# A gated attention kernel: the sums of the softmax inverted in another layout, a sixth subtraction on VectorE, and another order of the prologue

## The reference

```python
xn = (x - mean(x)) / sqrt(var(x) + 1e-5)              # over the 128 columns
Q, K, V = xn @ Wq, xn @ Wk, xn @ Wv                   # 16 heads of 64
A = softmax(Q K^T / 8) V                              # per batch and head
P = gelu(A) @ Wpost
s = xn + P
g = silu(quantised(xn) @ quantised(ffn_w).T + bias)   # blocks of 32, FP6 grid
out = x + s * g
```

## Time and profile before

| What | Value |
|---|---|
| median of 3 runs | 1389.54 us (1388.74 to 1390.49) |
| the profiled execution | 1389.97 us, span of its instructions 1388.2 us |
| TensorE busy | 1351.9 us, 97% |
| VectorE busy | 1129.9 us, 81% |
| GpSimd busy | 1152.7 us, 83% |
| ScalarE busy | 766.7 us, 55% |
| mean granted TensorE clock | 0.994 |

### The profile page before, as it was taken

The page is one execution under the profiler, slowest core; times in us unless marked ns, Lnnn a source line. Parts: engine busy times, 40 slices in busy tenths (PEclk is TensorE's granted clock), DMA queues, the critical chain, the costliest instruction groups (busy, mean ns, idle before and its releaser), DMA issues.

```text
span 1388.2 us, 25953 instructions
## 1 busy us (share of the span) xinstructions
PE 1351.9 (97%) x9810; PEld 736.2 (53%) x9810; DVE 1129.9 (81%) x1563; ACT 766.7 (55%) x1059; POOL 1152.7 (83%) x548
## 2 busy tenths in 40 slices
PE   5899999999999999999999999999999999999998
PEld 2455555555455555555555454555555455555588
DVE  6688888888888888888888898888888888888633
ACT  2355556555556665555556556555555555555583
POOL 1488899889889889888988899898889889988850
PEclk9999999999999999999999999999999999999999
DMA  2011112111111112211111111121111101122284
GB/s 81 17 41 53 52 58 77 42 61 58 58 48 65 55 42 66 69 51 54 64 56 42 64 56 57 48 64 56 42 64 56 47 28 49 63 66 70 84 272 130
DMA packets 70551, 87.60 MB, mean 63 GB/s; under 512 B 30494, under 2 KB 44574, under 8 KB 70428
## 3 DMA queue, kind: packets, MB, share of 16 engines
q1 hardware_dynamic: 70428, 85.95, 19.3%
HBM read 69.66 MB, written 16.25 MB: 62 GB/s over the span
## 4 chain that ended last, share of the span: by engine, by line
PE 88%; DVE 9%; issue 1%; ACT 1%; DMA 0%; POOL 0%; SPq 0%
PE acc L523 29%; PE scores L504 23%; PE peaks L483 12%; PE extra L406 9%; PE scores L513 5%; DVE half_maxes L942 5%; PE extra L419 4%; PE scores L587 4%; PE extra L447 1%; PE extra L454 1%; DVE extra L909 1%; DVE quant_tmp L908 1%; DVE turned_sums L985 0%; ACT x_in L618 0%; PE extra L429 0%
## 5 line engine op out<-in xcount | busy, mean ns | idle before, releaser
L825 POOL TENSOR_TENSOR prob_sum<-prob_sum,probs 128x1024 f32<-128x1024 f32 x384 | 914.7, 2382 | 89.0 <-ACT probs L702 48.0
L942 DVE TENSOR_REDUCE half_maxes<-peaks 128x2 f32<-128x1024 f32 x504 | 616.4, 1223 | 170.1 <-PE peaks L483 164.6
L702 ACT ACTIVATE probs<-scores 128x1024 f32<-128x1024 f32 x357 | 355.2, 1024 | 489.2 <-PE scores L513 485.9
L523 PE MATMUL acc<-probs,vals 128*64 128x512 f32 x2048 | 486.1, 595 | 0.0
L523 PEld LDWEIGHTS acc<-probs,vals 128*64 128x64 f32 x2048 | 139.0, 137 | 234.7 <-issue 225.2
L483 PE MATMUL peaks<-k_hi,q_hi 64*128 64x512 f32 x1008 | 231.9, 455 | 8.9 <-DVE half_maxes L942 8.8
L825 POOL TENSOR_TENSOR prob_sum<-probs 128x1024 f32<-128x1024 f32 x64 | 153.4, 2397 | 87.1 <-ACT probs L702 87.1
L483 PEld LDWEIGHTS peaks<-k_hi,q_hi 64*128 64x128 f32 x1008 | 95.2, 184 | 213.4 <-issue 142.4
L504 PE MATMUL scores<-q_hi,k_hi 64*128 64x512 f32 x1024 | 203.1, 393 | 0.0
L504 PE MATMUL scores<-q_hi,k_lo 64*128 64x512 f32 x1024 | 202.5, 392 | 0.0
L504 PE MATMUL scores<-q_lo,k_hi 64*128 64x512 f32 x1024 | 202.1, 391 | 0.0
(11 more groups left out here) (155 smaller groups left out, 947.1 us busy)
## 6 DMA issues: line engine op xcount, KB each, us to landing
max_rep<-max_scratch SPq DMA_DIRECT2D x62, 512.0 KB, 4.0
inv_sum<-inv_scratch SPq DMA_DIRECT2D x128, 128.0 KB, 2.8
att_scratch<-att SPq DMA_DIRECT2D x48, 256.0 KB, 2.1
probs<-att_scratch SPq DMA_DIRECT2D x8, 512.0 KB, 5.9
max_scratch<-turned SPq DMA_DIRECT2D x252, 1.0 KB
xTs<-att_scratch SPq DMA_DIRECT2D x4, 512.0 KB, 3.5
out_dram<-xn SPq DMA_DIRECT2D x8, 256.0 KB, 3.2
max_rows<-max_scratch SPq DMA_DIRECT2D x126, 2.0 KB
```

The lines of the kernel that those rows point to most:

```text
L523: last = mm(acc[own[h], :], vals[(s // 2) % 2][:, j, own[h]], probs[j][:, h, :], start=(k == 0), stop=(k == KT - 1), tile_position=col[h])
L702: sa.activation(probs[j][:, :, :], src[:, :, :], ACT.Exp, scale=DH ** -0.5).then_inc(probs_ready, 1)
L825: gp.tensor_tensor(prob_sum[s % 2][:, :, :], before[:, :, :], probs[order(s)[j]][:, :, :], ALU.add).then_inc(probs_summed, 1)
L942: v.tensor_reduce(half_maxes[:, :, f // 2, f % 2], peaks[:, :, :], AX.X, ALU.max).then_inc(peaks_read, 1)
```

## The change: what it does

- `BY_VECTOR` gets (0, 4) for odd steps: VectorE also subtracts the maxima of tile 4, in round 2, so six tiles a pair are its own. TensorE leaves out the L513 pair of that tile, and ScalarE takes tile 5 before tile 4.
- The sums lie in SBUF eight to a partition over 128 partitions, not 32 to a partition over 32: the transpose (L981) and its semaphore are gone, the load is two transfers of 64 partitions, each in pieces of 8 values, the addition runs over 128x32 to 128x8 and the inversion over 128x8. The inverses come back in another order, and GpSimd reads them 16 values apart in `normalise`.
- `centre` and `gates` move to the odd step: `centre` in two parts of four tiles, at the end of rounds 2 and 3, and `gates` at the end of round 2, with the following `high` of q put ahead of the second exponential of round 3. `square` moves to round 0 of the next pair's even step.
- The prologue: TensorE runs 18 matmuls on constants into `peaks` before its first transpose; its first peaks and the projections of v are interleaved; VectorE normalises the first half of rows as early as it can, with the weight's blocks and quantisation in the gaps, and reduces four peaks before it makes the lower parts of the second half.

```diff
...
-    sum_d = nc.dram_tensor("sum_scratch", (P // SQ, 2 * HALF // SQ, SQ), F32, kind="Internal").ap()
+    sum_d = nc.dram_tensor("sum_scratch", (2, P // SQ, SQ, HALF // SQ), F32, kind="Internal").ap()
...
-    BY_VECTOR = ((0, 2, 4, 6), (0,))
+    BY_VECTOR = ((0, 2, 4, 6), (0, 4))
...
-        sums, turned_sums = sb("sums", [P, P]), sb("turned_sums", [P, SQ])
-        group_sums, sums_turned, sums_flat = sums[:, 0:SQ], turned_sums[:, :], turned_sums[0:SQ, :]
+        group_sums, sums = sb("group_sums", [P, 2 * HALF // SQ]), sb("sums", [P, P // SQ, 2 * HALF // P])
+        sums_flat = sb("sums_flat", [P, 2 * HALF // P])
...
-        group_summed, folded = sem("group_summed"), sem("folded")
+        group_summed = sem("group_summed")
...
+        N_WARM = 18
...
-                sp.wait_ge(folded, s + 1)
-                above(sp, sums_loaded, 16 * s)
-                sp.dma_start(sum_d.rearrange("g b i -> (g b) i"), sums_turned).then_inc(sums_stored, 16)
+                sp.wait_ge(group_summed, s + 1)
+                above(sp, sums_loaded, 32 * s)
+                sp.dma_start(sum_d.rearrange("h g i b -> (g i) h b"), group_sums[:, :].rearrange("p (h b) -> p h b", h=2)).then_inc(sums_stored, 16)
-                sp.dma_start(sums[0:SQ, :].rearrange("b (g i) -> b g i", g=P // SQ), sum_d.rearrange("g b i -> b g i")).then_inc(sums_loaded, 16)
+                for h in (0, 1):
+                    sp.dma_start(sums[own[h], :, :], sum_d[h].rearrange("g i b -> g (i b)").rearrange("g (r c) -> r g c", r=DH)).then_inc(sums_loaded, 16)
-                sp.dma_start(inv_d.rearrange("h (b i) -> (h b) i", i=SQ), sums_flat).then_inc(inv_stored, 16)
+                sp.dma_start(inv_d.rearrange("h (r c) -> (h r) c", r=DH), sums_flat[:, :]).then_inc(inv_stored, 16)
...
-            def project_v(use):
+            def project_v(use, tiles=range(QT)):
-                for t in range(QT):
+                for t in tiles:
-                last.then_inc(filled, 1)
+                if tiles[-1] == QT - 1:
+                    last.then_inc(filled, 1)
...
+            pe.wait_ge(consts_set, N_SET)
+            for _ in range(N_WARM):
+                mm(peaks[:, 0, :], ones_r[:, :], max_rows[0][:, :], start=True, stop=True)
+            pe.wait_ge(xT_ready, 2)
+            first_peak(1)
+            first_peak(2)
-            for i in range(1, 6):
+            pe.wait_ge(lows_ready, 2)
+            for i in range(3, 7):
-            pe.wait_ge(lows_ready, 4)
-            project_v(("v", 0, 0))
-            first_peak(6)
-            project_v(("v", 0, 1))
+                project_v(("v", 0, 0), range(i - 3, i - 2))
+            project_v(("v", 0, 1), range(0, 1))
-            pe.wait_ge(consts_set, N_SET)
+            project_v(("v", 0, 1), range(1, QT))
...
-            def centre(p):
-                b, t0, nt = parts[p]
-                act.wait_ge(means_ready, p + 1)
-                for t in range(t0, t0 + nt):
+            def centre(b, part):
+                act.wait_ge(means_ready, part_of(b, 0) + 1)
+                for t in range(4 * part, 4 * part + 4):
-                last.then_inc(centred, 1)
+                if part == 1:
+                    last.then_inc(centred, 1)
...
+                gates_now = n % HP == 1 and n > 1
+                    if n + 2 < NP and half == 1 and r == 3 and gates_now:
+                        high(("q", n + 2, 0))
...
-                    if n + 2 < NP and half == 1 and r == 3:
+                    if n + 2 < NP and half == 1 and r == 3 and not gates_now:
...
-                    if half == 0 and r == 3 and n % HP == 1 and n > 1:
+                    if half == 1 and r == 2 and gates_now:
-                        if half == 0 and r == 3 and n % HP == 2:
+                        if half == 1 and r == 2 and n % HP == 2:
-                            centre(part_of(later, 0))
-                        if half == 1 and r == 2 and n % HP == 2:
+                        if half == 1 and r > 1 and n % HP == 2:
+                            centre(later, r - 2)
+                        if half == 0 and r == 0 and n % HP == 3:
...
-                gp.tensor_tensor(att[p % HP][:, halves[s % 2]], raw[s % 2][:, :], inv[s % 2][:, :], ALU.mult).then_inc(normalised, 1)
+                by_32 = lambda a: a.rearrange("p (b i) -> p b i", i=SQ)
+                gp.tensor_tensor(by_32(att[p % HP][:, halves[s % 2]]), by_32(raw[s % 2][:, :]),
+                                 inv[s % 2][:, :].rearrange("p (i b) -> p b i", i=SQ), ALU.mult).then_inc(normalised, 1)
...
+                above(dve, sums_stored, 16 * s)
+                v.tensor_reduce(group_sums[:, :], prob_sum[s % 2][:, :, :].rearrange("p h (b i) -> p (h b) i", i=SQ), AX.X, ALU.add,
+                                apply_transpose=True).then_inc(group_summed, 1)
+            def invert_sums(s):
+                dve.wait_ge(sums_loaded, 32 * (s + 1))
-                v.tensor_reduce(group_sums, prob_sum[s % 2][:, :, :].rearrange("p h (b i) -> p (h b) i", i=SQ), AX.X, ALU.add,
-                                apply_transpose=True).then_inc(group_summed, 1)
-                dve.wait_ge(group_summed, s + 1)
-                v.transpose(sums_turned, group_sums).then_inc(folded, 1)
-            def invert_sums(s):
-                dve.wait_ge(sums_loaded, 16 * (s + 1))
-                v.tensor_reduce(sums_flat, sums[0:SQ, :].rearrange("b (g i) -> b i g", g=P // SQ), AX.X, ALU.add).then_inc(combined, 1)
+                v.tensor_reduce(sums_flat[:, :], sums[:, :, :].rearrange("p g c -> p c g"), AX.X, ALU.add).then_inc(combined, 1)
-                v.reciprocal(sums_flat, sums_flat).then_inc(flat_inverted, 1)
+                v.reciprocal(sums_flat[:, :], sums_flat[:, :]).then_inc(flat_inverted, 1)
-            for p in (0, 1):
-                sum_squares(p)
-            for p in (0, 1):
-                invert_root(p)
-            for p in (0, 1):
-                scale_first(p)
+            def quantise_w(part):
+                quantise(0, part, ffn_in, ffn_wq, ffn_wT[:, :], quant_T[:, :], NT, w_quantised)
+            dve.wait_ge(consts_set, N_SET)
+            sum_squares(0)
-            dve.wait_ge(consts_set, N_SET)
-            for part in range(4):
-                quantise(0, part, ffn_in, ffn_wq, ffn_wT[:, :], quant_T[:, :], NT, w_quantised)
+            invert_root(0)
+            sum_squares(1)
+            scale_first(0)
+            invert_root(1)
+            quantise_w(0)
+            scale_first(1)
+            for part in range(1, 4):
+                quantise_w(part)
-            first_reduce(0)
+            for i in range(4):
+                first_reduce(i)
-            for i in range(1, 8):
+            for i in range(4, 8):
```

## The result

The changed kernel takes 1393.78 us as a median of eight runs (1390.34 to 1396.29), the kernel before 1389.74 (1388.74 to 1391.16): a ratio of 1.0025, 95% interval 1.0014 to 1.0036. It is slower by 4.0 us, where 1.6 us less was forecast. A second set of five runs gave 1394.58 against 1389.57, 1.0037 (1.0023 to 1.0050).

What follows compares the result with a forecast made beforehand. The prediction took TensorE (busy 97%) as the bound, with VectorE level with it in round 2 of odd steps. Its terms, -7.5 - 4.6 - 1.0 + 11.5 = -1.6, took 1389.54 to 1387.9 us; range 1382 to 1396.

Steps and rivals of the forecast that it cites:

- prologue, to the end of the maxima: Prologue: earlier reciprocal and warmed clock bring the last maxima result from 33.27 to 25.8 us, -7.5; bounds -4.8 and -9.5.
- step 0: Step after the prologue: no change counted; TensorE staying at the higher clock there was only the good bound, -9.5 with the prologue.
- `centre`: Odd steps: moving it ends three waits of TensorE for ScalarE's copy of v, -4.6 us, with 0 as bad bound.
- gates: Moved ScalarE work that held up a TensorE load by 0.94 us three times: between 0 and -2.8, taken as -1.0.
- sixth subtraction with the shorter inversion: Odd steps, round 2: VectorE delays round 3's first peak; 24 steps lose 0.30 us and 7 lose 0.61, +11.5 in all.
- late sums in even steps: Longer sum transfers: 0, as only the tail's inversions wait; +15 us if each even step's inversion were half a microsecond late.
- round 3 gives nothing back: Odd steps, round 3: VectorE's two parts and its reduction end 0.04 us before the second peak asks.
- the free subtraction: Rival, round 2 of odd steps: VectorE isn't the bound, so the sixth subtraction costs nothing; -20.2, 1369.3 us; 8%.
- The clock at the higher level through step 0: Rival: TensorE's clock stays up through step 0 and round 2's stalls are a little shorter; -4 to -6, 1384.5 us; 16%.
- The slower rival: Rival, round 1 of odd steps: inversion over 128 partitions no shorter, all 31 steps lose 0.61; +5.8, 1395.3 us; 14%.
- The rival of half a prologue gain: Rival, prologue: interleaved peaks and v wait for each other, half of its gain is gone; 1391.6 us; 6%.
- `normalise` above 2.64 us: Rival: GpSimd's `normalise` takes over 2.64 us and GpSimd then sets the step; above 1400 us; 4%.

Runs made afterwards that it cites:

- e12: The changed kernel unaltered, run once more for the profile of an ordinary execution: 1394.58 us, the profiled execution 1393.49.
- e5: The kernel before with the new prologue alone: 1385.87 us against 1390.10, ratio 0.9968.
- e8: The changed kernel with the sixth subtraction in tile 6 (round 3) and the odd step's fold moved from round 3 to round 0: 1391.63 us, ratio 1.0014.
- e7: The kernel before with ScalarE's moved work alone (centre, square, gates and the q copy): 1384.41 us against 1390.10, ratio 0.9962.
- e1: The changed kernel with five subtractions a pair, as before, instead of six: 1374.53 us against 1390.55 for the kernel before, ratio 0.9884.
- e2: The kernel before with the sixth subtraction alone: 1410.85 us, ratio 1.0147.
- e13: The changed kernel with early fold, part 3 of the quantisation first, and 14 matmuls on constants between the first peaks: 1364.54 us, ratio 0.9821.
- e3: The kernel before with the new layout of the sums, eight to a partition, alone: 1383.89 us, ratio 0.9954.

## Why the prediction was wrong

The time up to the end of step 61 can be told apart step by step, on the ordinary profile of the changed kernel (e12) against the kernel before:

| Term | Forecast | Measured |
|---|---|---|
| prologue, to the end of the maxima | -7.5 | -6.4 (-6.6 in the first profile) |
| step 0 | 0 | +1.5 (-0.4 in the first profile) |
| `centre` | -4.6 | -4.8 |
| gates | -1.0 | -1.0 |
| sixth subtraction with the shorter inversion | +11.5 | +13.5 |
| late sums in even steps | 0 | +0.8 |
| sum | -1.6 | +3.6 |

- **The sixth subtraction.** The mechanism was right: VectorE full in round 2, a head-of-line wait at round 3's first peak, more lost than freed. The term was under-sized by 2 us: 0.36 to 0.38 us per ordinary odd step in place of 0.30, 0.72 in place of 0.61 for the six. Step 13 went from 19.01 to 19.41 (0.40, a little more than most). Its round 3's first peak comes at 9.55 in place of 9.50, which is 0.05 of the error. The rest lies in "round 3 gives nothing back": it gives 0.07 away, with 5.29 us from its first peak to the next step's (321.81 in the timeline) where it was 5.22. The prediction looked only at whether the second peak is kept waiting, and it isn't. What comes later is the projection of q behind it, released by part 3 of the quantisation: it starts 0.38 us behind the second peak (318.70 to 319.08), 0.32 in the kernel before (323.47 to 323.79).
- **The prologue with step 0.** This is the step with the largest error, and the one whose reasoning failed: -4.9 where -7.5 was forecast (e5: -4.2 as a median). The first reduction comes at 15.1 to 15.4 us, as forecast (15.3). The maxima end at 26.6 to 26.9 us, 6.4 to 6.6 us earlier: 0.9 to 1.1 short of the -7.5, since the last peak waits behind pieces of v and the clock. The step from there to the end of step 0 was taken as unchanged, with the clock only on the good side (-9.5). It takes 1.5 us more in e12, and up to 2.5 more (e5): a fall of the clock that lay ahead of the end of the maxima now lies in part behind it, where TensorE sets the time. A bound on the bad side of this term was missing, and it was the side that came true. The other assumption, that the warming holds until the projections, failed in one profile of ten.
- **The sums.** This step failed too: +0.8 where 0 was forecast. "So 0" rested on no wait outside the tail in the trace of before. That row tells that nothing was late, not by how much it was early. In the kernel before the sums had landed 0.7 to 1.7 us (mostly 1.5) before the addition asked; the two longer transfers (2.1 us to landing in place of 1.7), one behind the other, took 1.1 or more of it, and the 0.3 to 0.6 left is less than what landings vary by. The moved fold of e8 cures it: no wait outside the tail.
- **`centre`, the gates, `square`, `normalise`:** right, shown by e7 and by the rows of GpSimd. The stepped read cost 0.26 us, a fifth. The Trainium skill's rule (half as much again, "GPSIMD Engine Reference", section 7) has the direction right; the measured 1.54 us decides against the estimate of 1.92 that was worked out from it.
- **The sign and the range.** The range held the median, but the sign came out wrong. Three terms erred the same way: 2.6 us in the prologue with step 0, 2.0 in the sixth subtraction, 0.8 in the sums. No one of them turns the sign back: with the prologue as forecast the sum would still be +1.0, with the sixth subtraction as forecast +1.6. The forecast sum of -1.6 was smaller than the errors of the two large terms in it (-7.5 and +11.5), so its sign was worth little.

The rivals: the free subtraction is ruled out (e1, e2). The clock at the higher level through step 0 did not come in any of the profiles; e13 comes nearest, with matmuls added for it. The slower rival was named for an inversion that is no shorter; it is shorter (e3), so its 1395.3, 1.5 us from the median, is near it by luck. Its neighbour in the same line, late sums, was there, at 1 us and not 15. The rival of half a prologue gain (1391.6) has the size nearly right (4.2 of 7.5 by e5), but named peaks and v that wait for each other; they take about 1 us, and the rest is step 0's clock. `normalise` above 2.64 us is ruled out by its 1.54.

## What to carry to other kernels

Follow the engine that shares a round with the bound row by row before moving work to it: its mean share over the span (82% in the changed kernel) says nothing about the round in which it is full, and one instruction of 1.2 us a step there cost 20 us net of the 7 it freed. If it must go in, make its time in the same stretch first (the fold moved to a round with idle time), and ask what stands behind it in the queue and who waits for that (the quantisation that frees a bank). Where a transfer is made longer, read how early it lands, not only that nobody waits. Where a stretch is made shorter, ask whether what follows it stays as it was: here a fall of the clock moved into it.

The kernel with the early fold, part 3 first and the matmuls in the gaps takes 1364.54 us, 25 us under the kernel before and 30 under the changed one, both beside it on the same chip.

## What the runs showed of the hardware

- Matmuls ahead of the first real work do raise TensorE's clock (the projections behind them take 1.1 us in nine profiles, 1.97 in the kernel before), but in one profile of this prologue, with 1.9 us without work between, they ran at the lower level again (1.8 and 2.0 us).
- Matmuls on constants in the gaps of a stretch that VectorE bounds (e13) kept the granted clock at 1.00 from 20 to 30 us, where it was 0.50 from 25 to 30 in the changed kernel, and were worth 3.0 us by two profiles, 1.7 by the medians, behind that stretch.
- In step 0, 3.2 us more went with some 7 us more at the lower level (31.09 us at a granted 0.95, 34.28 at 0.85).
- Two executions of the same kernel with the same waits of TensorE (1.32 and 1.41 us) had different clocks behind them (granted 1.00 and 0.69 from 45 to 50 us).
- VectorE's addition with 32 values a partition takes 0.20 us and the inversion of 8 takes 0.20, against 0.35 and 0.34 (at 316.44 in the kernel before) for 128 and 32 values on a quarter of the partitions: with as many values in all, the time goes down with the values per partition, but not in proportion (a quarter of the values, 0.57 to 0.59 of the time).
